# Attention stage of a fused network: all stores of a sequence's operand parts ahead of the thirteen reads of its stacks

## What is computed

```python
xn = layer_norm(x, in_ln_w, in_ln_b)
proj = xn @ W_in.T + b_in
q, k, v, p, y = jnp.split(proj, [D_EXP, 2*D_EXP, 3*D_EXP, 4*D_EXP], axis=-1)
k = (1 - smear) * k + smear * k_prev
pos = jnp.cumsum(jax.nn.sigmoid(y).transpose(0, 2, 1), axis=-1)
scores = q/s @ (k/s).T / sqrt(16) + causal - (pos_i - pos_j)
attn = softmax(scores); o = attn @ v
out = layer_norm(silu(p) * o @ W_out.T)
```

## Time and profile before

| what | us |
|---|---|
| three runs of the kernel | 1697.78, 1703.57, 1704.34; median 1703.57 |
| the profiled execution, its own time | 1702.95 |
| its span, first to last instruction | 1701.2 |
| mean granted TensorE clock over the span | 0.659 of full speed |
| PE busy | 1393.9 (82%) |
| DVE busy | 1141.0 (67%) |
| ACT busy | 706.9 (42%) |
| POOL busy | 435.3 (26%) |

### The profile page before, as it was taken

One profiled execution on the slowest core, in us unless ns is written; L12 is line 12 of the kernel. 1 busy time (PEld: TensorE's weight loads), 2 busy tenths in 40 slices (PEclk: granted clock), 3 DMA queues, 4 the chain that ended last, 5 costly groups with the idle time before them and its releaser, 6 DMA issues. The chain is left out here.

```text
span 1701.2 us, 65489 instructions
## 1 busy us (share of the span) xinstructions
PE 1393.9 (82%) x27355; PEld 1028.8 (60%) x27370; DVE 1141.0 (67%) x5594; ACT 706.9 (42%) x2475; POOL 435.3 (26%) x818
## 2 busy tenths in 40 slices
PE   5788888888888888888888874689899898888887
PEld 4677777777777776777777762345555554544443
DVE  5767777777777777777777774456566576565475
ACT  3333232222222222222222220247676676665765
POOL 2011111111111111111111112362552552421354
PEclk6555555555555555555555555689999999998898
DMA  5200000000000000000000000573573573661001
GB/s 118 25 4 5 7 5 5 7 5 5 6 5 5 6 5 7 5 5 7 5 5 6 5 7 8 116 113 55 88 96 51 88 91 49 94 85 12 1 14 37
DMA packets 67597, 53.69 MB, mean 32 GB/s; under 512 B 11343, under 2 KB 67047, under 8 KB 67303
## 3 DMA queue, kind: packets, MB, share of 16 engines
q1 hardware_dynamic: 65126, 49.31, 19.0%
q10 hardware_dynamic: 2176, 0.20, 0.1%
HBM read 31.84 MB, written 15.47 MB: 28 GB/s over the span
## 5 line engine op out<-in xcount | busy, mean ns | idle before, releaser
L731 PE MATMUL PS<-GB,W 128*128 128x8 f16 x18432 | 575.2, 168 | 178.2 <-DVE GB L1041 174.0
L731 PEld LDWEIGHTS PS<-GB,W 128*128 128x128 f16 x18432 | 532.1, 104 | 286.8 <-DVE GB L1041 282.0
L2286 DVE TENSOR_REDUCE MX<-PS 128x1 f32<-128x512 f32 (+3 forms) x352 | 221.0, 636 | 181.1 <-PE PS L1805 180.0
L935 ACT ACTIVATE tr<-PS 128x16 f32<-128x16 f32 x512 | 93.7, 183 | 490.3 <-PE PS L731 490.3
L2054 ACT ACTIVATE PT<-PS 128x512 f32<-128x512 f32 (+1 forms) x352 | 193.2, 564 | 162.5 <-PE PS L1821 157.3
L937 ACT ACTIVATE tz<-PS 128x16 f32<-128x16 f32 x512 | 93.7, 183 | 193.0 <-PE PS L731 193.0
L1802 PE MATMUL PS<-KS,QS 99*128 99x256 bf16 (+3 forms) x512 | 137.7, 321 | 43.4 <-DMA KS<-k_parts 31.3
L1027 DVE SCALAR_TENSOR_TENSOR u_<-tr,PS 128x16 f32<-128x16 f32 x512 | 87.8, 172 | 124.4 <-PE PS L731 112.7
L685 POOL TENSOR_TENSOR rt<-mv,eps 128x1 f32<-128x1 f32 x96 | 18.2, 190 | 553.7 <-DVE mv L1052 553.7
L1034 DVE SCALAR_TENSOR_TENSOR zg<-tz,HR 128x16 f32<-128x16 f32 x512 | 90.2, 176 | 80.4 <-ACT tz L937 80.3
L1818 PE MATMUL PS<-QS,KS 102*128 102x256 bf16 (+3 forms) x512 | 134.0, 313 | 5.2 <-ACT PT L2054 2.6
(11 more groups left out here) (393 smaller groups left out, 2506.8 us busy)
## 6 DMA issues: line engine op xcount, KB each, us to landing
QS<-q_parts SPq DMA_DIRECT2D x42, 256.0 KB
KS<-k_parts SPq DMA_DIRECT2D x42, 256.0 KB
q_parts<-PQ SPq DMA_DIRECT2D x16, 384.0 KB, 13.0
k_parts<-PK SPq DMA_DIRECT2D x16, 384.0 KB, 14.0
X<-XM SPq DMA_DIRECT2D x32, 64.0 KB
out_dram<-X SPq DMA_DIRECT2D x8, 256.0 KB, 2.3
XM<-in_L_attn_x_dram SPq DMA_DIRECT2D x16, 80.0 KB
s_hh<-in_L_attn_w_hh_dram SPq DMA_DIRECT2D x1, 768.0 KB, 5.5
```

The source lines that it names most:

```text
L731: return pe.matmul(bank[:, p, at:at + B], W[:, kc, w:w + P], state[:, part, kc, :], start=False, stop=True, skip_group_check=True)
L935: act.activation(as_states(tr), now(pR), ACT.Tanh, scale=gate_scale).then_inc(hn_tr.sem, 1)
L2286: dve.tensor_reduce(MX[:, g % 2, heads[0]:heads[-1] + 1, NT - 1 - it], p_x[:, k % 2, 0:len(heads) * w].rearrange("p (a w) -> p a w", w=w), ...
```

## The change

SP's list for sequences 1 to 7 is put in another order. The two k stores and all three waits for landed stores stand ahead of the wait on `e_ps`, and the thirteen reads are issued in one run behind it, the extra rows first. The number and size of the DMAs, and all other engines' programs, stay as they are. `project_first` is not changed.

```diff
                     sp.dma_start(one(ad[at]), KAT[:, :]).then_inc(a_out.sem, 16)
-                    if not (isinstance(b, int) and b < 2):
-                        sp.wait_ge(e_ps.sem, sp.snap(b * (NI * NG4) - NI * NG4))
-                    sp.wait_ge(q_out.sem, q_out.value(sp, b))
-                    for r, part in enumerate((0, 0, 0, 1, 1, 2)):
-                        sp.dma_start(QS[r * DH:(r + 1) * DH, p, :, :], head_rows(qd, part)).then_inc(stack_in[p].sem, 16)
                     for c in range(2):
                         sp.wait_ge(parts_k.sem, parts_k.value(sp, b, 4 * (c + 1)))
                         sp.dma_start(one(kd[at])[:, c * P:(c + 1) * P, :].rearrange("s p n -> p s n"),
                                      PK[:, c, :, :]).then_inc(k_out.sem, 16)
+                    sp.wait_ge(q_out.sem, q_out.value(sp, b))
                     sp.wait_ge(a_out.sem, a_out.value(sp, b))
+                    sp.wait_ge(k_out.sem, k_out.value(sp, b))
+                    if not (isinstance(b, int) and b < 2):
+                        sp.wait_ge(e_ps.sem, sp.snap(b * (NI * NG4) - NI * NG4))
                     sp.dma_start(KS[96:KF, p, :, :], one(ad[at]).rearrange("(h r) n -> r h n", r=6)).then_inc(stack_in[p].sem, 16)
-                    sp.wait_ge(k_out.sem, k_out.value(sp, b))
+                    for r, part in enumerate((0, 0, 0, 1, 1, 2)):
+                        sp.dma_start(QS[r * DH:(r + 1) * DH, p, :, :], head_rows(qd, part)).then_inc(stack_in[p].sem, 16)
                     for r, part in enumerate((0, 1, 2, 0, 1, 0)):
                         sp.dma_start(KS[r * DH:(r + 1) * DH, p, :, :], head_rows(kd, part)).then_inc(stack_in[p].sem, 16)
```

## The result

The changed kernel takes 1675.75 us in the median of four runs (1673.36 to 1677.33); the kernel before, 1703.95 beside it (1697.78 to 1706.33). The ratio is 0.984, with a 95% interval of 0.981 to 0.987: 28 us faster. The forecast was 1674, in 1665 to 1689.

What follows compares the result with a forecast made beforehand. PE was taken to lead, losing time to late KS reads and the clock's fall behind those waits. Gains 19.5 + 9.9 + 3.6 less 3.65 give 29.35 us off 1702.95, 1673.6; forecast 1674, range 1665 to 1689.

Steps and rivals of the forecast that it cites:

- The mechanism: SP's reads into KS come late because the k stores and their landing lie between the two halves of the reads.
- R: SP's first read issue to PE's release: 14.8 + 0.8 + 15.0 = 30.6 us, range 29.7 to 32.4.
- Sequences 1 to 5: PE's waits for KS reads, 21.05 us in all, shrink to 1.5 us: gain 19.5 us.
- The clock: Behind PE's waits in sequences 1 to 5, short waits leave the clock up: gain 9.9 us.
- Sequence 6: PE's wait at slot 22 falls from 10.2 to 6.6 us, gain 3.6; the clock falls as before.
- Sequence 0: Reads of sequence 1's stacks now follow both k stores: new PE wait 2.65 us plus 1.0 for clock, cost 3.65.
- What was costed at nothing: DVE and ACT keeping pace, earlier q stores behind queued reads, and thirteen issues of 6.2 us hidden behind bytes: no cost.
- rival A: Queues don't keep order, so next q stores share engines with the reads: 6 to 7 us off, 1697; chance 6%.
- B: POOL or DVE becomes PE's wait at slot 22 and after, halving the gain in sequences 1 to 5: 1689; 14%.
- C: One long run of reads slows the engines or issue; at 95 GB/s 1726 us, slower; chance 3%.
- D: Nothing changes, PE's release being set by something other than the store's detour: 1703 us; chance 3%.

Runs made afterwards that it cites:

- a3_first_new: Kernel before with only sequence 1 given the new list, the loop over sequences 2 to 7 keeping the old; 1706.66 us against 1704.10, ratio 1.0013.
- a1_again: The changed kernel again, no edit, for a second profile; 1675.65 us, ratio 0.983.
- a0_before: The kernel before again, no edit, for a second profile; one run, 1702.40 us.
- a4_stores_only: Against the kernel before, only the two k stores moved ahead of `e_ps`, reads in their old order with waits between; 1675.99 us, ratio 0.983.
- b2_halves: Changed kernel with each of the thirteen reads cut in two by heads, the first half issued once its heads are free; 1660.57 us, ratio 0.974.

## Why the prediction was right

**The mechanism** held as stated, and two runs show both sides of it: the stores moved without the rest give the whole gain, the run of reads with the stores still behind `e_ps` gives none.

**R, the time from the first issue to PE's release.** Forecast 30.6 us, with 29.7 to 32.4. After, it is 1215.30 - 1184.16 = 31.1 in sequence 1 and 1512.21 - 1480.63 = 31.6 in sequence 6; over the five with a wait the mean is 31.5 (31.1, 31.7, 31.2, 31.9, 31.6). The forecast is 0.9 below that mean, and in sequence 1 the rows say which term it was. The rate changes from that of reads to that of stores at about 1213.0 (stretches below), T + 28.9, which is where the sum had the end of the reads' bytes: 30.6 less the 1.6 us from 1212.5 to 1214.13 is 29.0. PE's release comes 2.3 us behind that, not 1.6. So the bytes came as forecast, and what was too small is the time from the end of the bytes to the release. In quarter-us stretches of sequences 2 to 4 it is 2.6 to 2.8 us, against 1.4 to 2.4 in sequences 1 to 5 of the kernel before. Why it is longer behind one long run no run shows.

**Sequences 1 to 5.** 1.5 us of waits was left in the forecast, 3.4 measured: gain 17.7, not 19.5.

**The clock.** 9.9 forecast, 8.8 measured as what the waits leave over, 9.0 as PE's busy time. Waits of 0.5 to 1.2 us leave the clock up in this kernel: it is 1.00 over sequences 1 to 5, four of which have one. Waits well short of 4 us were followed by a fall to 0.50: 2.12 us in a3_first_new and 2.87 in a1_again (sequence 0), and 2.88 in a0_before (sequence 4).

**Sequence 6.** 3.6 forecast, 2.8 measured (7.42 us left and not 6.6), for R again. In a1_again 6.06 is left, with R at 31.9, so PE's coming to slot 22 varies by more than the miss.

**Sequence 0.** 3.65 forecast. In the profile after, T is 4.4 us late: 0.84 of that lies ahead of the maxima at 1127.00 (1126.16 before), 3.6 behind; the 0.84 is not the change's, for a1_again, with the same list, has them at 1126.24. But the profile shows it as low clock and no wait, and only the second profile shows the 2.87 us wait. That it agrees in the first profile is partly luck: against the kernel before at a long low stretch (1126.18 to 1182.23, 56.1 us) it is 1.1 us, against the one at a short stretch (53.6 us) 3.6 and, with the wait, 57.82 - 53.58 = 4.2. The two terms show in that second profile. The reads went out at 1126.08 (forecast 1126.0), and R from there is 31.3. Behind the wait the granted clock is 0.50 from about 1158.4 to 1161.8 us, which costs at most 1.7 us, where 1.0 was put in. By the times of whole kernels it is 2.6 in both comparisons, neither of them clear of noise.

**What was costed at nothing** cost nothing. SP's issues grew to 12.7 us in place of the 6.2 forecast (below), still hidden behind the bytes. The queues kept order: the first q store, issued at 1198.45 with 14 us of reads still queued, shows in the rates only from 1213 on, as the short stretches after say:

```profile
1205.20:1206.20 1.00, 1.00 (x11) 1.00 1.14 114
...
1212.20:1213.20 1.00, 1.00 (x22) 1.00 1.14 143
1213.20:1214.20 1.00, 1.00 (x14) 1.00 1.14 305
```

So rival A fell. B fell as well: behind slot 22 nothing longer than 0.34 us stands in PE's timeline of sequences 1 to 5. C fell by the rate: 119 GB/s over 1185.7 to 1213.0. The terms add to 29.35 forecast and 25.6 in the profiled pair; the medians differ by 28.2. The spans of the second profiles, a0_before and a1_again, are 1700.7 and 1673.3 and differ by 27.4, so a single pair is good to some 2 us. D fell with the waits.

## What to carry to other kernels

A store that the next reads need, put between two sets of reads in an ordered queue, costs its bytes, its landing and the queue's idle time; a wait of 4 us cost nearly 2 us more here, since TensorE's clock fell behind it; first look whether the data were ready long before. Then ask what the reads themselves wait for: here a buffer freed by heads, in two steps, took away all that the reordering had left, and made the reordering needless. Where two stretches of a trace differ in clock, compare with a second profile before a difference of 2 to 4 us is given to the change.

## What the runs showed of the hardware that I had not expected

**SP's issue slowed down behind a long queue.** In one run of thirteen, the extra rows and six reads into QS are issued in 3.6 us, but the next six into KS take 9.12 us in place of 2.81. The same in a4_stores_only (8.05 us), where the order is another. The last is taken at about T + 12.9, when at 114 GB/s some 1.4 of 3.2 MB have moved: an estimate of 1800 rows of 1 KB still queued. In b2_halves, where each set has half of the bytes in as many DMAs, the six into KS take 2.75 us again (rows at 1223.04 above), so it is not the number of DMAs. That it is the amount queued is my reading. It cost nothing here, since the queues had work and SP had nothing else to do, but it is 6 us in which SP issues nothing else.

**The clock in the record and the matmuls of the GRU.** Two of the ten profiles show a mean granted clock of 0.98 and 0.97 over the span, where all others show 0.65 to 0.66. Other executions do so too, and their times are no different: in a3_first_new six of the twelve do, with a median of 1707.0 us, against 1706.3 for the other six. In a4_stores_only the GRU's stretch stands at 1.00, in the changed kernel at 0.50, with the same busy time, here of the changed kernel:

```profile
150.00:1050.00 900.00, 729.22 (x20273) 630.01 (x20272) 651.89 (x4021) 257.17 (x1470) 151.19 (x355) 0.50 0.02 6
```

and of a4_stores_only:

```profile
150.00:1050.00 900.00, 728.65 (x20255) 629.39 (x20252) 651.67 (x4015) 257.16 (x1468) 151.88 (x357) 1.00 0.02 6
```

The mean matmul of line 731 is 168 ns in both. Whether the clock really was at another level there, and the small matmuls do not feel it, or the record is wrong in one of them, these runs do not say. In the attention the level does show: the maxima's 512-column matmul is listed with 0.39 us at 1.00 and 0.61 us at 0.50 in the timelines above. Ends of matmuls are modelled there, but starts say the same: the next matmul starts 0.43 us later at 0.50 (1121.64 and 1122.07 in the kernel before) and 0.22 us later at 1.00 (1216.32 and 1216.54 in the changed kernel).
